# Local attention stage: eight sequences written out in place of a loop over pairs, and the first norm applied by GpSimd with its statistics one slot sooner

## The reference, cut to what matters

```python
def _L2_attn_ref(x, ...):                  # x is _layernorm(previous x, axis=-1)
    h = _layernorm(x, ln_g, ln_b)
    lin_out = _linear_attention(h @ wq_lin + bq_lin, h @ wk_lin + bk_lin, h @ wv_lin + bv_lin)
    win_out = _window_attention(h @ wq_loc + bq_loc, h @ wk_loc + bk_loc, h @ wv_loc + bv_loc, rel_bias)
    gate_in = jnp.concatenate([lin_out, win_out, h], axis=-1)
    gate = jax.nn.sigmoid(jnp.maximum(gate_in @ wg1 + bg1, 0.0) @ wg2 + bg2)
    out = gate * lin_out + (1.0 - gate) * win_out
    return out @ wo + bo + x
...
x = x + _L2_attn_ref(_layernorm(x, axis=-1), ...)
```

## Time and profile before

| what | before |
|---|---|
| median of three runs | 2634.88 us (2629.48 to 2635.00) |
| the profiled execution's own time | 2637.11 us |
| its span in the profile | 2635.3 us |
| mean granted TensorE clock | 0.971 |
| busy: PE, DVE, ACT, POOL | 94%, 73%, 61%, 44% |
| the stage, from its first scores to the next stage's first product | 1704.90 to 1964.38 us |

### The profile page before, as it was taken

The page is one execution under the profiler, slowest core; times in us unless marked ns, Lnnn a source line. Parts: engine busy times, 40 slices in busy tenths (PEclk is TensorE's granted clock), DMA queues, the critical chain, the costliest instruction groups (busy, mean ns, idle before and its releaser), DMA issues. The chain is left out here.

```text
span 2635.3 us, 37625 instructions
## 1 busy us (share of the span) xinstructions
PE 2467.8 (94%) x11094; PEld 1405.0 (53%) x11094; DVE 1934.5 (73%) x3923; ACT 1616.5 (61%) x3503; POOL 1148.1 (44%) x924
## 2 busy tenths in 40 slices
PE   7999989899999999999989999988879998799988
PEld 5767754455555555555444444466644444456655
DVE  7888867799999999999966445466634444577754
ACT  4565533688888888888833344477744443466644
POOL 1000012599999999999930002022200001355442
PEclk8999989999999999999999999999989998999998
DMA  2000024344444444444443221000011110000000
GB/s 110 1 1 1 0 89 94 119 161 161 163 164 159 164 161 164 160 166 157 167 141 82 79 99 65 0 2 1 1 49 65 65 65 28 1 1 1 1 1 17
DMA packets 34771, 205.70 MB, mean 78 GB/s; under 512 B 4016, under 2 KB 5168, under 8 KB 13360
## 3 DMA queue, kind: packets, MB, share of 16 engines
q1 hardware_dynamic: 34608, 203.83, 22.0%
HBM read 201.19 MB, written 2.62 MB: 77 GB/s over the span
## 5 line engine op out<-in xcount | busy, mean ns | idle before, releaser
L1520 POOL TENSOR_TENSOR mam_state_c<-mam_state,weights_r 128x1024 f32<-128x1024 f32 x256 | 600.3, 2365 | 10.1 <-DVE mam_state L1482 8.3
L1482 DVE TENSOR_TENSOR_SCAN mam_state<-banks,mam_dbu 128x1024 f32<-128x1024 f32 x256 | 577.1, 2275 | 1.6 <-ACT banks L1551 0.7
L1601 PE MATMUL banks<-mam_state_c,identity 128*128 128x512 f32 x1024 | 485.0, 606 | 10.6 <-POOL mam_state_c L1520 9.8
L1551 ACT ACTIVATE banks<-mam_dt,mam_a_neg 128x255 f32<-128x255 f32 x1024 | 425.0, 461 | 63.7 <-DVE mam_state L1482 63.2
L1601 PEld LDWEIGHTS banks<-mam_state_c,identity 128*128 128x128 f32 x1024 | 187.2, 190 | 224.1 <-issue 189.2
L1027 PE MATMUL banks<-route_xnt,weights_r 128*128 128x512 f32 x512 | 243.3, 598 | 1.9 <-PEq L736 1.0
L1465 DVE TENSOR_TENSOR mam_dbu<-banks,weights_r 128x1024 f32<-128x1024 f32 x192 | 227.5, 1198 | 0.0
L434 ACT ACTIVATE at_probs<-banks,at_nmax 128x256 f32<-128x256 f32 x256 | 117.9, 473 | 139.1 <-DVE at_nmax L375 139.1
L556 POOL TENSOR_SCALAR route_ln_rs<-route_ln_mv 128x4 f32<-128x4 f32 x16 | 5.1, 318 | 449.3 <-DVE route_ln_mv L634 449.3
L2710 POOL TENSOR_TENSOR at_attention<-at_relu 128x512 f32<-128x512 f32 x128 | 131.2, 1042 | 127.4 <-ACT at_relu L2755 79.7
L975 DVE TENSOR_TENSOR m2b_hidden<-m2b_gelu,m2b_comb_spread 128x512 f32<-128x512 f32 x120 | 80.7, 690 | 116.4 <-ACT m2b_gelu L1005 113.8
(11 more groups left out here) (433 smaller groups left out, 5012.3 us busy)
## 6 DMA issues: line engine op xcount, KB each, us to landing
weights_r<-mam_bc_rows SPq DMA_DIRECT2D x128, 1024.0 KB, 4.7
m2a_comb_spread<-m2a_comb_rows SPq DMA_DIRECT2D x15, 1024.0 KB, 8.0
m2b_comb_spread<-m2b_comb_rows SPq DMA_DIRECT2D x15, 1024.0 KB, 8.0
m1a_comb_spread<-m1a_comb_rows SPq DMA_DIRECT2D x14, 512.0 KB, 6.9
m1b_comb_spread<-m1b_comb_rows SPq DMA_DIRECT2D x14, 512.0 KB, 7.5
weights_r<-in_mb SPq DMA_DIRECT2D x1, 4332.0 KB, 12.9
weights_r<-in_m SPq DMA_DIRECT2D x1, 4200.0 KB, 12.8
weights_r<-in_a SPq DMA_DIRECT2D x1, 2632.0 KB, 10.7
```

What stands on the lines that cost most here:

```text
L1482: dve.tensor_tensor_scan(flat2(h[:, i % 4, :, :, :]), decay(i), flat2(dbu[:, i % 4, :, :, :]), 0.0, ALU.mult, ALU.add).then_inc(h_ready, 1)
L1520: pool.tensor_tensor(hc[:, j % 4, :, :, :], h[:, j % 4, :, :, :], c_rows(j), ALU.mult).then_inc(hc_ready, 1)
L1551: i = act.activation(decay(j)[:, o + 1:o + S], dt[:, q, c, 1:S], ACT.Exp, scale=aneg[:, l, k:k + 1])
L1601: k = pe.matmul(y_bank(q)[:, :], K.ident[:, :], flat(hc[:, j % 4, n, :, :]), start=(j == 0 and n == 0), stop=(j == NP - 1 and n == 1))
```

## The change

A new helper `over_each_sequence` calls the slots of all eight sequences with plain numbers, for all four engines of this stage; the loop, its two branches back and the register arithmetic are gone from it. The other stages keep theirs. VectorE's statistics of the first norm move from slot 2 to slot 1. GpSimd applies the first norm itself, behind its power, in slot 2; VectorE's application and its wait for `x_ready` are gone. VectorE's statistics and GpSimd's work of the second norm move from slot 4 to slot 6. The calls for sequence 0 in the expert stage keep their places.

```diff
@@ -278,6 +278,16 @@
     main((B - 1, 1), (B - 2, 0), None)
     for i in range(tail):
         slot(i, None, (B - 1, 1), None)
+
+
+def over_each_sequence(slot, slots, tail):
+    for s in range(B):
+        now, last = (s, s % 2), (s - 1, 1 - s % 2) if s else None
+        nxt = (s + 1, 1 - s % 2) if s + 1 < B else None
+        for i in range(slots):
+            slot(i, now, last, nxt)
+    for i in range(tail):
+        slot(i, None, (B - 1, (B - 1) % 2), None)
 
 
 def lagged(i, lag, slots, now, last):
@@ -1699,13 +1709,9 @@
 
 
 def window_vector(K, A, dve, i, s, q):
-    if i == 2:
-        xs = lambda j: K.x[:, bass.ds(s * W + j * P, P)]
-        window_statistics(A.N, dve, xs, chain(dve, A.dve_s))
-        if not (isinstance(s, int) and s == 0):
-            dve.wait_ge(A.x_ready, s)
-        norm_apply(A.N, dve, xs, s)
-    if i == 4:
+    if i == 1:
+        window_statistics(A.N, dve, lambda j: K.x[:, bass.ds(s * W + j * P, P)], chain(dve, A.dve_s))
+    if i == 6:
         link = chain(dve, A.dve_s)
         dve.wait_ge(A.N.xn, s + 1)
         window_statistics(A.M, dve, lambda j: A.N.out[:, j * P:(j + 1) * P], link)
@@ -1731,7 +1737,12 @@
 def window_gpsimd(K, A, pool, i, s, q):
     if i == 2:
         norm_pool(K, A.N, pool, s)
-    if i == 4:
+        pool.wait_ge(A.N.rstd, s + 1)
+        for j in range(TS):
+            k = pool.tensor_scalar(A.N.out[:, j * P:(j + 1) * P], K.x[:, bass.ds(s * W + j * P, P)],
+                                   A.N.mv[:, j, 0:1], A.N.rs[:, j:j + 1], ALU.subtract, ALU.mult)
+        k.then_inc(A.N.xn, 1)
+    if i == 6:
         link = chain(pool, A.pool_s)
         pool.wait_ge(A.M.stats, s + 1)
         pool.sem_inc(A.pool_hold, 1)
@@ -1821,9 +1832,9 @@
         dve.sem_inc(A.blocks_made, 1)
     if (p, e) == (2, 12):
         dve.wait_ge(added, 1)
-        window_vector(K, A, dve, 2, 0, 0)
+        window_vector(K, A, dve, 1, 0, 0)
     if (p, e) == (2, 14):
-        window_vector(K, A, dve, 4, 0, 0)
+        window_vector(K, A, dve, 6, 0, 0)
     if (p, e) == (3, 2):
         window_vector(K, A, dve, 10, 0, 0)
     if (p, e) == (3, 3):
@@ -1861,7 +1872,7 @@
     link(pool.affine_select(out=A.band, in_=A.band, compare_op=ALU.is_ge, fill=-1e30, base=2 * A.HALF,
                             pattern=[[0, A.H], [-1, A.BW]], channel_multiplier=1))
     pool.sem_inc(A.masked, 1)
-    for i in (2, 4, 8, 13):
+    for i in (2, 6, 8, 13):
         window_gpsimd(K, A, pool, i, 0, 0)
 
 
@@ -2015,7 +2026,7 @@
                         route_vector(K, ahead, dve, 0, AHEAD[i])
                 dve.memset(pr[:, :, :, :], 0.0).then_inc(pr_clear, 1)
                 dve.wait_ge(masked, 1)
-                over_sequences(dve, slot, H, TAIL)
+                over_each_sequence(slot, H, TAIL)
 
             @block.gpsimd
             def _(pool):
@@ -2040,7 +2051,7 @@
                         prepare(i, *nxt)
                     if now and not nxt and i == 3:
                         route_gpsimd(K, ahead, pool, 0)
-                over_sequences(pool, slot, H, TAIL)
+                over_each_sequence(slot, H, TAIL)
 
             @block.scalar
             def _(act):
@@ -2087,7 +2098,7 @@
                     if not now and i == 1:
                         route_scalar(K, ahead, act, 0, "combt")
                 act.wait_ge(pr_clear, 1)
-                over_sequences(act, slot, H, TAIL)
+                over_each_sequence(slot, H, TAIL)
 
             @block.tensor
             def _(pe):
@@ -2208,7 +2219,7 @@
                                 k = pe.matmul(K.ps[6][:, j * P:(j + 1) * P], ot[:, j * P:(j + 1) * P], f("wo"),
                                               start=True, stop=True)
                             k.then_inc(y_ps, 1)
-                over_sequences(pe, slot, H, TAIL)
+                over_each_sequence(slot, H, TAIL)
 
             K.clear_retired(block)
         A.end(K)
```

## The result

The changed kernel takes 2615.21 us (median of 7 runs, 2614.28 to 2623.64) against 2634.88 (7 runs, 2629.48 to 2635.05). The medians are 19.7 us apart. The ratio over all runs is 0.9935 with a 95% interval of 0.9925 to 0.9945: 17 us less, between 14.5 and 19.8. One of the seven new runs took 2623.64, the other six at most 2615.4. The profiled execution took 2615.19 us.

What follows compares the result with a forecast made beforehand. The prediction took TensorE's chain of work to bound the windowed attention stage, holes from other engines paid in full. 10.0 + 2.9 + 1.4 = 14.3 us off 2634.88 gave 2621; own range 2616 to 2626, eight in ten 2614 to 2629.

Steps and rivals of the forecast that it cites:

- Rival one: Second norm reaches TensorE's slot 8 late and takes back the 0.49 us; only branches gain, 2625 us; chance 0.15.
- Rivals two: VectorE's branch stall is only partly removed or reappears elsewhere, such as a later loop; 2625.6 us; chance 0.14.
- three: Straight code starves VectorE at each of sequences 3 to 7, making the kernel slower; 2646 us; chance 0.04.
- four: The loop is not the cause of VectorE's stall, so only 4.3 us go; 2630.6 us; chance 0.09.
- The branches, 10.0 us: Writing out the windowed attention stage's loop removes about 5 us each at sequences 3 and 5, clock loss included.
- the first stage's 0.8 us: Alternative price for two branches, from the first stage, where a branch back costs TensorE only 0.39 us.
- The norm, 0.49 us for each of six sequences: Windowed attention: new norm order closes TensorE's holes at head 3 and the window output; 2.9 us, ends 0 and 3.4.
- The 0.13 to 0.22 us that sequences 2, 4 and 6 took more: Windowed attention: excess over sequence 1, cause not shown, left in by the forecast (0 to 0.6 us).
- Sequence 0, 1.4 us: Windowed attention: 0.73 us of TensorE's wait for head 3 plus 0.7 us of statistics go; ends 0.5 and 2.
- The cover of the second norm, 0.0 to 0.4 us: Windowed attention, slot 8: second norm ready by 1748.8 to 1749.2, TensorE wants it at 1749.2.
- GpSimd's application under cover: Windowed attention, slot 2: GpSimd applies the first norm in 1.59 us against VectorE's 0.60, hidden by 4.5 us of cover.

Runs made afterwards that it cites:

- e3: The changed kernel with the loop over pairs put back on VectorE alone; ratio 0.9960 to the kernel before.
- e4: The changed kernel with the loop put back on TensorE and ScalarE, VectorE and GpSimd written out; ratio 0.9928 to the kernel before.
- e10: The kernel before with a loop of two passes in this stage, sequences 5 and 6 written out; ratio 0.9989 to the kernel before.
- e2: The kernel before with only the loop written out on all four engines, norm order as it was; ratio 0.9955 to the kernel before.
- e8: The changed kernel with the first attention stage also written out on VectorE, ScalarE and TensorE; median 2621.92 us, ratio 0.9946 to the kernel before.
- e1: The changed kernel with the loop put back on TensorE, VectorE and ScalarE, GpSimd staying written out; ratio 0.9964 to the kernel before.
- e7: The changed kernel with the second norm one slot later, in slot 7; ratio 0.9967 to the kernel before.
- e6: The changed kernel with VectorE applying the first norm in slot 2 again, the rest of the new order kept; ratio 0.9937 to the kernel before.
- e9: The kernel before with the norm's new order alone, VectorE applying the first norm, loops on all engines; ratio 0.9962 to the kernel before.

## Why the prediction was right

The forecast was 2621 with a range of 2614 to 2629; measured 2615.2. The direction and the mechanism held: both 33 us distances went, nothing new appeared in sequences 3 to 7, and VectorE's branch is shown to be the cause (e3, e4, e10). Rival one, no gain from the norm, fell with e2 against the profile after (28.27 to 27.55). Rivals two, three and four fell with e2 and the profile after, which shows no issue wait over 1 us of VectorE or ScalarE behind the stage either. The gain was put at 14.3 us; the sum fell by 16.3, the runs by 17 (14.5 to 19.8). That the total came so close is in part luck: the norm and sequence 0 gave more than forecast, and the largest term slightly less. Term by term:

- **The branches, 10.0 us.** With the old order: 33.03 - 28.27 and 33.11 - 28.27 (e2), 9.6 us. Taking the price at these very branches was right; the first stage's 0.8 us would have misled. The prediction counted the clock into the price without saying how much of it that is: by e3, more than half at its second branch and nothing at its first. So the 5 us are no fixed price of a branch; with the new order's shorter stalls it was 1.6 to 4.5 us.
- **The norm, 0.49 us for each of six sequences.** Against written-out sequences it is 0.72 (28.27 to 27.55). The step was mis-sized because it took sequence 7 against sequence 1 inside the loop, 28.07 us, while sequence 1 written out with the old order takes 28.27, where TensorE waits 0.42 us for head 3 instead of 0.17 (the row below, from e2); why it waits longer there is not shown. Against the loop the reading held: from slot 0 to L2173 sequence 1 now takes 1736.96 - 1725.98 = 10.98 us, what sequence 7 took before. The 0.13 to 0.22 us that sequences 2, 4 and 6 took more, left in by the prediction, also went. Against the earlier trace rows, sequences 1, 2, 4 and 6 became shorter by 0.52, 0.74, 0.73 and 0.64 us.

```profile
1736.70 0.83 PE L2118 MATMUL banks<-at_k_masked,at_q 32*128 32x160 f32 x16 [0.42 <-DVE at_negated_max L1979]
```

- **Sequence 0, 1.4 us.** It shortened by 2.64, above the upper bound of 2. The prediction counted waits and left the clock out. In every profile TensorE's clock is low for a part of this sequence, and two things vary: where it falls and how long it stays down. Below are the 2 us behind slot 0 in e2 (old order) and in e8 (new order), then the stretch from 10 to 18 us behind slot 0 in the kernel before, in the changed one and in e2.

```profile
1702.93:1704.93 2.00, 2.00 (x20) 1.67 (x20) 1.15 (x1) 0.00 (x0) 0.00 (x0) 0.57 0.02 4
...
1705.64:1707.64 2.00, 2.00 (x20) 1.67 (x20) 1.53 (x1) 0.00 (x0) 0.00 (x0) 0.57 0.00 0
...
1714.90:1722.90 8.00, 6.68 (x53) 4.22 (x53) 4.00 (x24) 4.49 (x12) 3.95 (x6) 0.59 0.00 0
...
1709.78:1717.78 8.00, 5.46 (x56) 3.80 (x56) 5.58 (x33) 6.03 (x17) 3.96 (x6) 1.00 0.01 2
...
1712.93:1720.93 8.00, 5.14 (x55) 3.75 (x56) 5.11 (x32) 5.80 (x16) 3.94 (x6) 1.00 0.00 0
```

In e2 and e8 the clock falls at the same place, in the first 2 us (0.57), and in both it is back by 10 us: 26.65 - 25.79 = 0.86 us is what the order is worth there, inside the range of 0.5 to 2. In the kernel before and in the changed one it is still 1.00 over those first 2 us and falls later. Then the new order has it back by 10 us (26.20; e1 26.28), while the old order has 0.59 from 10 to 18 us (28.84; e10 28.81, at 0.60). So of the 2.64 us about 0.9 are waits, and the rest goes with a clock that stays low longer. That the old order's holes keep it low rests on two profiles, and in a run where the clock falls early, as in e2, that part of the gain is absent. The prediction also checked the second norm's cover for sequence 1 alone; here L149 waits 0.41 us.
- **The cover of the second norm, 0.0 to 0.4 us.** Measured 0.45; rival one was near. e7 shows that 0.8 us beyond it costs 0.84 us per sequence.
- **GpSimd's application under cover.** Right, 1.59 us for the pair as forecast, and read only at 1737.31. But the prediction counted VectorE's 1.27 us stall and 0.60 us of work as part of the gain. e6 gives the same distances with VectorE applying: statistics one slot earlier and the second norm two slots later carry all of it.

## What to carry to other kernels

Look for "issue" waits that come once per pass of a loop, and price them by the distance between equal marks of ordinary and first sequences of a pass, not by the stall: here one engine's 4.5 us stall cost 5 us, in another stage 2 us cost 0.3, and the branches of the other engines were free. Read TensorE's granted clock at such a place too: behind nearly equal stalls it went with most of the difference between 1.6 and 4.5 us. Before handing work to another engine, try moving it by a slot on its own; a statistic one slot earlier did what the hand-over was thought to do. And a step has its slot: of four places for the second norm slot 6 is the best, and slot 5 is worse than slots 4 and 6 on either side of it.

## What the runs showed of the hardware that I had not expected

Nearly equal idle times of TensorE before the same product had three different ends. Behind 1.66 us in e3 the granted clock stayed at 1.00 and the sequence lost 1.6 us; behind 1.66 us in e1 it was 0.79 over 8 us, for 3.2 us; behind 1.82 us in e3's other pass 0.63, for 4.5. Their history differs slightly (the transposes just ahead had waited 0.32, 0.42 and 0.48 us); which of this decides is not shown. And VectorE's stall behind a branch had a second part of 0.56 to 0.72 us (e1, e3) or of 1.5 to 1.7 (before, e9, e10), the long one wherever VectorE applied the norm; in e1 and e3 GpSimd's loop was gone as well. The Trainium skill ("Runtime: NRT & Kernel Launch", Instruction fetch mechanics) explains a stall behind a taken branch by a fetch, where the target lies outside the stretch of code that the engine holds. e3 and e10 agree that VectorE's stall follows the branch. In e4, with branches on TensorE and ScalarE, neither has an issue wait over 0.7 us, and the sum is that of the changed kernel. No run here shows the fetch itself, or whether their targets lay inside that stretch.
